# A graph-attention layer on one core: the edge stage works two steps ahead, with the masks prepared behind the copy of turned probabilities

## The chip, the cores and the metric

The kernel runs on one core of a Trainium2 chip. The core has five engines that run their own instruction streams and wait for each other through semaphores: TensorE (PE, matmuls and transposes into the PSUM banks), VectorE (DVE), ScalarE (ACT), GpSimd (POOL) and SyncE (SP, here for DMAs and counting). The metric is the device time of one execution in microseconds (us), as the median of several runs.

## What is computed

Cut to what matters:

```python
h = relu(layernorm(x))                       # x: 6250 x 256, float32
q, k, v = h @ wq + bq, h @ wk + bk, h @ wv + bv
scores = sum(q[dst] * k[src], -1) * scale + edge_weight * we + be   # 200000 edges, dst sorted
exp_s = exp(scores - segment_max(scores, dst)[dst])
attn = exp_s / segment_sum(exp_s, dst)[dst]
out = segment_sum(v[src] * attn[:, None], dst)
y = layernorm(h + out + h @ ws + bs)
y = layernorm(y + gelu(y @ w_ff1 + b_ff1) @ w_ff2 + b_ff2)
return x + y
```

The edges are sorted by destination. wk is folded into q and wv is applied after the sums, so that an edge needs only the row h[src].

## The kernel before

The kernel has three stages. The first normalises x, writes h to DRAM and builds q for 49 blocks of 128 nodes, each as three bfloat16 parts (`q3`). It also makes a table of steps. The third does wv, the residual, both layer norms and the feed-forward part.

Between them lies the edge stage. A chunk is 512 edges (J = 4 groups of 128 partitions), 392 chunks in all. A step is one pair of a chunk and a node block whose edges it holds; there are 440 steps here, run as 55 trips of U = 8 steps, written out in the loop body. Tiles that alternate are indexed by k = u % 2.

What each engine does for step s before the change (S, M, T, E name groups of TensorE's work):

- GpSimd gathers h rows by `src`, four indirect DMAs for each chunk (L488), into a ring of 8 slots (`rows`). SyncE counts landed chunks and, from `summed`, frees slots (L372).
- VectorE: `mark` (L705) writes `onehot[k]`, the 0/1 mask of edge against node, from the destinations. `edge_scores` (L832) multiplies the expanded q in banks 0 to 3 with the gathered rows and sums each row into a dot product, four instructions, then adds the edge term (L838). A custom instruction (L886) subtracts the mask from the scores spread in bank 4 and takes the maximum (`masked`, `new_max`). `add_sums` (L845) scales the running sums `acc` of the previous step's block and adds the new ones.
- ScalarE: `decay` and `probsT` are exponentials of `masked` (L618, L619). When TensorE has turned the probabilities, it copies them from banks 4 and 5 in two halves (L622). `prepare` (L585) turns `onehot[k]` into `outside`, 0 inside and -1e30 outside.
- TensorE: T turns `probsT` (L1066, 4 transposes), E expands q by the mask of step s+2 into banks 0 to 3 (L1011, 12 matmuls, in two halves), S spreads the scores of step s+1 into bank 4 (L1017, 4 transposes), M sums the rows of step s weighted by the probabilities (L1079, 4 float32 matmuls, which the profile shows as 8 passes).

Order in a step. TensorE: T, first half of E, S, second half of E, M. VectorE: masking of s, scores of s+1, keep the maximum, mark of s+3, read the old maximum (L709), add the sums of s-1. ScalarE: exp of s, two copies, prepare of s+2. S waits for the first of ScalarE's two copies (`probs_done`), since bank 4 holds half of the turned probabilities. The mark of s+3 waits until `outside_done` is at least s+2, which is the preparation of step s+1, one that ScalarE did in its step s-1.

Once per trip the residual projection of one block (`turn_h`, `copy_hTe`, `project_h`, `copy_r`, `store_r`) is done in the right half of bank 5. The order is the order of the code: each engine's queue is in order, and there is no scheduler.

Of the kernel before, what the change touches and what calls it, by code (L numbers as in the profile page):

```python
# [6 lines left out]
BF16 = mybir.dt.bfloat16  # L7
I32 = mybir.dt.int32
I16 = mybir.dt.int16
ALU = mybir.AluOpType  # L10
# [3 lines left out]
P = 128  # L14
# [8 lines left out]
BLOCKS = 64  # L23
# [10 lines left out]
def gnn_layer(nc, x, src, dst, edge_weight, wq, bq, wk, bk, wv, bv, ws, bs, we, be, g1, b1, g2, b2,  # L34
# [31 lines left out]
    ROUND = TP * BLOCKS + 1  # L66
    assert D == 2 * P and REST > 0 and FULL % 4 == 0 and B * P < PAD_DST and B < BLOCKS and S == G
# [3 lines left out]
    with ctx:  # L71
# [27 lines left out]
        stats = sb("stats", [P, NB, 6])  # L99
        mean = sb("mean", [P, NB])  # L100
        rstd = sb("rstd", [P, NB])
        nmr = sb("nmr", [P, NB])
        tmp = sb("tmp", [P, NB])
# [7 lines left out]
        ew_all = sb("ew_all", [P, R + J])  # L111
# [6 lines left out]
        WORK = 11120  # L118
# [148 lines left out]
        masked = part(C)  # L267
        probsT = masked
        probs = part(C).rearrange("p (j n) -> p j n", j=J)
        product = part(J * (D1 + 1) // 2, BF16).rearrange("p (j n) -> p j n", j=J)  # L270
# [3 lines left out]
        dots, score = (part(2 * J).rearrange("p (k j) -> p k j", k=2) for _ in range(2))  # L274
        old_max = part(2)
        new_max = part(1)
        decay = part(2)
# [6 lines left out]
        onehot_done, outside_done, q_edges, dotted, scored = sem("onehot_done"), sem("outside_done"), sem("q_edges"), sem("dotted"), sem("scored")  # L284
        spread, max_read, masked_done, max_kept = (sem(n) for n in ("spread", "max_read", "masked_done", "max_kept"))
        exp_done, turned, probs_done, summed, added = (sem(n) for n in ("exp_done", "turned", "probs_done", "summed", "added"))

        def counts(eng):
# [3 lines left out]
            n = eng.snap(regs[0], min_val=NW, max_val=TRIPS)  # L292
            m = eng.snap(regs[1], min_val=0, max_val=1)
            return n, m, eng.snap(regs[2], min_val=1, max_val=B)
# [10 lines left out]
        def block_of(eng, step):  # L305
            return eng.snap(eng.to_reg(step & (BLOCKS - 1)), min_val=0, max_val=B)

        def chunk_of(eng, step):
            return eng.snap(eng.to_reg(step >> (BLOCKS.bit_length() - 1)), min_val=0, max_val=B * TP + U)

        def slot_of(eng, chunk):
            return eng.snap(eng.to_reg(chunk & (S - 1)), min_val=0, max_val=S - 1)

        with nc.Block() as block:
            @block.sync
            def _(sp):
# [42 lines left out]
                with sp.Fori(0, rounds) as r:  # L359
                    with sp.Fori(0, NW) as i:  # L360
# [3 lines left out]
                        for u in range(G):  # L364
# [4 lines left out]
                            used_up = sp.to_reg(sp.snap(regs[u], min_val=1, max_val=T + B + S) + r * TP)  # L369
# [3 lines left out]
                            if u % WC == 0:  # L373
                                window = trip * 2 + (u // WC + 1)
                                before, marks = sp.to_reg(window * 16), sp.to_reg(sp.snap(regs[u + WC - 1], min_val=1, max_val=T + B + S) + r * TP)
# [7 lines left out]
                sp.sem_inc(chunk_landed, 1)  # L383
# [5 lines left out]
                all_back = sp.to_reg(sp.snap(all_turns, min_val=NW, max_val=B * NW) * 16 + 16)  # L389
                sp.wait_ge(late_in, 7 * 16)  # L390
                sp.wait_ge(r_copied, sp.to_reg(sp.snap(all_turns, min_val=NW, max_val=B * NW) + 1))
# [114 lines left out]
            def _(act):  # L506
# [51 lines left out]
                for b in range(B):  # L558
# [10 lines left out]
                    if b == 16:  # L569
                        act.wait_ge(ws_in, 3 * 16)  # L570
                        act.wait_ge(tab_turned, 3)
                        nc.scalar.activation(ew_all[:, R:R + J], banks[6][:, 0:J], ACT.Identity, bias=wb[:, 1:2], scale=wb[:, 0:1])
                        edge_terms(0, 512, 6, tab_copied)
                        edge_terms(512, 512, 7, tab_copied)
# [13 lines left out]
                nc.scalar.activation(decay[:, 1:2], eps[:, 0:1], ACT.Exp, scale=0.0).then_inc(sums_set, 1)  # L588
# [7 lines left out]
                def copy_hTe(turn):  # L596

                    act.wait_ge(hTe_ready, turn + 1)
                    nc.scalar.copy(hT_e, banks[5][:, D:2 * D]).then_inc(hTe_copied, 1)
                    act.dma_start(h_in, h_rows[bass.ds((turn + 1) % B * P, P), :]).then_inc(h_back, 16)  # L600

                def copy_r(turn):

                    act.wait_ge(r_stored, turn * 16 + 16)
                    act.wait_ge(r_ready, turn + 1)
                    nc.scalar.copy(r_out, banks[5][:, D:2 * D]).then_inc(r_copied, 1)

                def store_r(turn):

                    act.wait_ge(r_copied, turn + 2)  # L610
                    act.dma_start(r_rows[bass.ds(turn % B * P, P), :], r_out).then_inc(r_stored, 16)

                def trip(r, i, steps):
                    first = act.snap(act.to_reg(r * TP + i * U), min_val=0, max_val=B * TP)
                    for u in range(steps):
                        s, k = first + u, u % 2
                        act.wait_ge(masked_done, s + 1)
                        nc.scalar.activation(decay[:, k:k + 1], old_max[:, k:k + 1], ACT.Exp, bias=new_max, scale=-1.0)  # L618
                        nc.scalar.activation(probsT, masked, ACT.Exp, bias=new_max, scale=-1.0).then_inc(exp_done, 1)  # L619
                        for half in (1, 0):  # L620
                            act.wait_ge(turned, s * 2 + (2 - half))
                            nc.scalar.copy(probs[:, 2 * half:2 * half + 2, :].rearrange("p j n -> p (j n)"), banks[5 - half][:, 0:2 * P]).then_inc(probs_done, 1)  # L622
                        prepare(s + 2, k)
                        for at, body in ((3, copy_hTe), (6, copy_r), (7, store_r)):
                            if steps == U and u == at:
                                body(act.snap(act.to_reg(r * NW + i), min_val=0, max_val=B * NW))
# [5 lines left out]
            def _(dve):  # L632
# [57 lines left out]
                held = dve.alloc_register("block_of_last_step")  # L690
                steps_done = dve.alloc_register("steps_done")
                dve.reg_mov(held, B)
                dve.reg_mov(steps_done, 0)
                def place_of_mark(step):

                    chunk = chunk_of(dve, step)
                    there = dve.to_reg((chunk >> 2) * 16 + 16)
                    at = dve.snap(dve.to_reg((chunk & (G - 1)) * C), min_val=0, max_val=(G - 1) * C)
# [14 lines left out]
                def mark_first_steps():  # L713
# [6 lines left out]
                    nc.vector.memset(banks[7][:, 0:D1], 0.0).then_inc(sums_set, 1)  # L720
                    dve.load(regs[0:3], steps_tab[0:1, 0:3])
                    ahead[:] = [dve.snap(v, min_val=0, max_val=TP * BLOCKS) for v in regs[0:3]]
# [8 lines left out]
                for b in range(B):  # L731
# [44 lines left out]
                    if b == PLAN + 13:  # L776
# [19 lines left out]
                        nc.vector.scalar_tensor_tensor(out=steps_tab[0:1, :], in0=row(row_k), scalar=float(BLOCKS), in1=row(row_b), op0=ALU.mult, op1=ALU.add).then_inc(plan, 1)  # L796
# [8 lines left out]
                    if b == PLAN + 17:  # L805
# [4 lines left out]
                        nc.vector.tensor_scalar(free_row[0:1, 0:most], free_row[0:1, 0:most], float(S - 1), is_sorted[0:1, 0:1], ALU.add, ALU.mult).then_inc(plan, 1)  # L810
                        dve.wait_ge(plan, 12)
                        nc.vector.scalar_tensor_tensor(out=free_tab[0:1, :], in0=free_row[0:1, 0:most], scalar=1.0, in1=srow[0:1, 0:most], op0=ALU.add, op1=ALU.add).then_inc(plan_done, 1)
# [10 lines left out]
                def edge_scores(step, r, s, k, meanwhile=None):  # L823
                    chunk = chunk_of(dve, step)
                    slot = slot_of(dve, chunk)
                    column = dve.snap(dve.to_reg((chunk - r * TP) * J), min_val=0, max_val=R)
                    there, first_half, second_half = dve.to_reg(chunk + 1), dve.to_reg(s * 2 + 1), dve.to_reg(s * 2 + 2)
                    dve.wait_ge(chunk_landed, there)
                    for half, ready in ((0, first_half), (1, second_half)):
# [617 lines left out]
```

## Time and profile before

| | before |
|---|---|
| time, median of 3 runs | 2334.37 us (2331.2 to 2334.62) |
| profiled execution, span | 3211.3 us |
| PE busy | 2427.3 us (76%) |
| DVE busy | 1767.6 us (55%) |
| POOL busy | 1635.5 us (51%) |
| ACT busy | 1193.2 us (37%) |
| mean granted TensorE clock | 0.921 of full speed |

The profiled execution's own time is its span of 3211.3 us; it is 877 us longer than the median of the runs without a profile. Its parts must be read with that in mind: shares and durations of single instructions come from it, the total comes from the runs. PEld is TensorE's loading of weights, which overlaps the matmuls. "Idle before" is the time in which an engine stood ahead of an instruction, with what released it: "remote" and "issue" mean that the profile shows no work that ended then. The chain that ended last lies almost wholly in the third stage and tells nothing of the edge stage.

### The profile page before, as it was taken

To read this page: it belongs to the slowest core of one execution; us is meant where nothing else is said; L and a number is where in the kernel's file an instruction comes from. 1 tells how busy PE (TensorE), PEld (TensorE's weight loads), DVE (VectorE), ACT (ScalarE), POOL (GpSimd) and SP (SyncE) were. 2 spreads that over 40 slices of the span, in tenths; PEclk is the share of its full clock that TensorE was granted. 3 is DMA by queue.
4 is the path that set the end of the run, shared out by engine and by line. 5 is a ranking of instruction groups with operands and counts; after the bars stand their busy time and mean duration, and the time that the engine had idled before them with its cause. 6 is when DMAs were issued, how large, how long until landed. Compare 5 with 4: busy or idle time off the path is not lost. (4 is left out here: it accounts for less than half of the span.)

```text
span 3211.3 us, 68474 instructions
## 1 busy us (share of the span) xinstructions
PE 2427.3 (76%) x14747; PEld 1996.1 (62%) x14748; DVE 1767.6 (55%) x7372; ACT 1193.2 (37%) x2930; POOL 1635.5 (51%) x1828
## 2 busy tenths in 40 slices
PE   7577677777777777777777777777777777778998
PEld 5455556556555556565656566665666666657897
DVE  7454455555555545554555555555555555556787
ACT  6333333333333333333333333333333333334666
POOL 5355565555555545555554555555555445441154
PEclk8898899899899989998998999899988899999999
DMA  7233333333233323333233333332333233222222
GB/s 231 76 103 103 99 105 101 103 98 107 90 100 100 96 86 101 97 98 96 90 102 92 96 90 96 96 98 87 96 96 100 87 92 95 83 93 71 82 74 68
DMA packets 148148, 311.29 MB, mean 97 GB/s; under 512 B 33566, under 2 KB 84625, under 8 KB 148104
## 3 DMA queue, kind: packets, MB, share of 16 engines
q0 software_dynamic: 75264, 205.62, 21.5%
q1 hardware_dynamic: 54718, 90.19, 8.6%
q10 hardware_dynamic: 18122, 14.96, 1.5%
q8 instruction: 20, 0.33, 0.0%
q14 instruction: 24, 0.20, 0.0%
HBM read 290.21 MB, written 20.43 MB: 97 GB/s over the span
## 5 line engine op out<-in xcount | busy, mean ns | idle before, releaser
L488 POOL DMA_INDIRECT work<-h_rows,idx x1536 | 1457.3, 949 | 1339.9 <-SPq L372 956.2
L1079 PE MATMUL bank<-work 128*128 x3520 | 939.0, 412 | 24.5 <-issue 17.7
L1011 PE MATMUL bank<-q,onehot 128*128 x5304 | 804.6, 291 | 1.2 <-DVE work L832 0.7
L1079 PEld LDWEIGHTS bank<-work 128*128 128x128 f32 x3520 | 700.1, 211 | 146.8 <-issue 45.2
L886 DVE CUSTOM_DVE_ANT_0 work<-bank,work 128x512 f32<-128x512 f32 x440 | 330.5, 751 | 778.7 <-remote 476.4
L622 ACT COPY work<-bank 128x256 f32<-128x256 f32 x880 | 295.0, 376 | 1182.6 <-remote 812.8
L832 DVE SCALAR_TENSOR_TENSOR work<-bank,work 128x257 bf16<-128x257 f32 x1764 | 651.6, 425 | 143.5 <-PE bank L1011 44.2
L1017 PE MATMUL bank<-ident,work 128*128 128x128 f32 x1764 | 307.4, 302 | 500.5 <-ACT work L622 313.3
L1011 PEld LDWEIGHTS bank<-q,onehot 128*128 128x128 bf16 x5304 | 549.5, 104 | 85.4 <-issue 1.7
L1017 PEld LDWEIGHTS bank<-ident,work 128*128 128x128 f32 x1764 | 212.8, 148 | 578.0 <-ACT work L622 442.4
L1066 PE MATMUL bank<-ident,work 128*128 128x128 f32 x1760 | 283.6, 285 | 191.8 <-ACT work L619 182.8
L1066 PEld LDWEIGHTS bank<-ident,work 128*128 128x128 f32 x1760 | 214.8, 145 | 277.2 <-ACT work L619 230.6
L618 ACT ACTIVATE work<-work 128x1 f32<-128x1 f32 x440 | 129.5, 294 | 674.5 <-DVE work L886 550.3
L845 DVE SCALAR_TENSOR_TENSOR acc<-acc,work,bank 128x257 f32 x441 | 212.1, 481 | 230.4 <-remote 156.9
L619 ACT ACTIVATE work<-work 128x512 f32<-128x512 f32 x440 | 311.5, 708 | 0.0
L585 ACT ACTIVATE work<-onehot 128x512 bf16<-128x512 bf16 x442 | 282.9, 640 | 0.0
L705 DVE TENSOR_SCALAR onehot<-dst_words,node 128x512 bf16 x443 | 163.2, 368 | 72.5 <-issue 44.3
L832 DVE DVE_READ_ACCUMULATOR work<-bank,work 128x1 f32 x1764 | 145.0, 82 | 0.0
L838 DVE TENSOR_TENSOR work<-work,ew_all 128x4 f32<-128x4 f32 x441 | 72.5, 164 | 107.4 <-DVE work L832 43.5
L1405 PE MATMUL bank<-work,dst_words 128*128 128x128 f32 x784 | 96.0, 275 | 0.5 <-DVE work L1308 0.5
L1413 PE MATMUL bank<-dst_words,work 128*128 128x256 f32 x392 | 92.6, 379 | 0.0
L1405 PEld LDWEIGHTS bank<-work,dst_words 128*128 128x128 f32 x784 | 91.5, 192 | 1.2 <-issue 0.5
(195 smaller groups left out, 1519.5 us busy)
## 6 DMA issues: line engine op xcount, KB each, us to landing
dst_words<-dst_short SPq DMA_DIRECT2D x99, 512.0 KB
work<-h_rows,idx POOLq DMA_INDIRECT x1568
bias<-h_rows ACTq DMA_DIRECT2D x56, 128.0 KB
r_rows<-bias ACTq DMA_DIRECT2D x55, 128.0 KB
work<-r_rows SPq DMA_DIRECT2D x49, 128.0 KB, 2.3
h_rows<-acc SPq DMA_DIRECT2D x12, 512.0 KB, 6.6
work<-in_x SPq DMA_DIRECT2D x12, 512.0 KB, 3.5
out<-work SPq DMA_DIRECT2D x48, 128.0 KB, 1.7
```

Source lines behind the costliest of these rows:

```text
L488: pool.indirect_dma_start(rows[:, u, j, 0:D], None, h_rows, bass.IndirectOffsetOnAxis(idx[:, half, u * J + j:u * J + j + 1], 0)).then_inc( ...
L585: nc.scalar.activation(outside[:, k, :], onehot[:, k].rearrange("p j n -> p (j n)"), ACT.Copy, scale=BIG, bias=-BIG).then_inc(outside_done, 1)
L619: nc.scalar.activation(probsT, masked, ACT.Exp, bias=new_max, scale=-1.0).then_inc(exp_done, 1)
L622: nc.scalar.copy(probs[:, 2 * half:2 * half + 2, :].rearrange("p j n -> p (j n)"), banks[5 - half][:, 0:2 * P]).then_inc(probs_done, 1)
L832: last = nc.vector.scalar_tensor_tensor(out=product[:, j, 0:D1], in0=banks[j][:, 0:D1], scalar=SCALE, in1=rows[:, bass.ds(slot, 1), j, :], ...
L845: nc.vector.scalar_tensor_tensor(out=a, in0=a, scalar=decay[:, k:k + 1], in1=banks[6 + k][:, 0:D1], op0=ALU.mult, op1=ALU.add).then_inc(ad ...
L886: nc.vector.tensor_tensor_reduce(out=masked, in0=banks[4][:], in1=outside[:, k, :], scale=-1.0, scalar=old_max[:, k:k + 1], op0=ALU.add, o ...
L1011: last = nc.tensor.matmul(banks[j][:, 0:D1], onehot[:, k, j, :], q3[:, bass.ds(b, 1), c, 0:D1], start=(c == 0), stop=(c == 2))
L1017: last = nc.tensor.transpose(banks[4][:, j * P:(j + 1) * P], score[:, k, j:j + 1].broadcast_to([P, P]), ident[:])
L1066: last = nc.tensor.transpose(banks[5 - half][:, j * P:(j + 1) * P], probsT[:, (2 * half + j) * P:(2 * half + j + 1) * P], ident[:])
L1079: last = nc.tensor.matmul(banks[6 + k][:, 0:D1], probs[:, j, :], rows[:, bass.ds(slot, 1), j, :], start=(j == 2), stop=(j == 1))
L1405: last = nc.tensor.matmul(banks[2 + place(b)][:, m * P:(m + 1) * P], w1_sb[:, c, m * P:(m + 1) * P], unit_T[:, place(b), c * P:(c + 1) * P ...
```

## The change

The edge stage is reordered so that VectorE scores step s+2 and marks step s+4 in step s, and the sums of a step are made one step later and added one step later still.

- TensorE in step s: S of s+1 (waits for `masked_done` of s, no longer for the copies), second half of M of step s-1, T of s (all four transposes into bank 5), both halves of E for step s+3, first half of M of step s-1.
- VectorE: masking of s, scores of s+2, mark of s+4, add the sums of s-2. `q_edges` and `dotted` have one semaphore for each half. The mark waits for `outside_done` of at least s+3, the preparation of step s+2. Chunk and block sit the other way round in the step table, which takes some register instructions from the loop.
- ScalarE: exp of s, where due a part of the residual's copies, one copy of all 512 columns from bank 5, prepare of s+2.
- `masked`/`probsT` and `probs` have two buffers, `decay` four columns; `onehot` and `outside` keep two.
- The residual projection uses spare columns of banks 6 and 7, in halves of 128 columns: four short copies at u = 2, 3, 5, 6 instead of two, and VectorE waits for them ahead of `add_sums` there. Slots of gathered rows are freed one step later.

```diff
-        masked = part(C)
+        masked = part(2 * C).rearrange("p (k n) -> p k n", k=2)
...
                         act.wait_ge(masked_done, s + 1)
-                        nc.scalar.activation(decay[:, k:k + 1], old_max[:, k:k + 1], ACT.Exp, bias=new_max, scale=-1.0)
-                        nc.scalar.activation(probsT, masked, ACT.Exp, bias=new_max, scale=-1.0).then_inc(exp_done, 1)
-                        for half in (1, 0):
-                            act.wait_ge(turned, s * 2 + (2 - half))
-                            nc.scalar.copy(probs[:, 2 * half:2 * half + 2, :].rearrange("p j n -> p (j n)"), banks[5 - half][:, 0:2 * P]).then_inc(probs_done, 1)
+                        nc.scalar.activation(decay[:, u % 4:u % 4 + 1], old_max[:, k:k + 1], ACT.Exp, bias=new_max, scale=-1.0)
+                        nc.scalar.activation(probsT[:, k, :], masked[:, k, :], ACT.Exp, bias=new_max, scale=-1.0).then_inc(exp_done, 1)
+                        if steps == U and u in (2, 3):
+                            copy_hTe(act.snap(act.to_reg(r * NW + i), min_val=0, max_val=B * NW), u - 2)
+                        if steps == U and u in (5, 6):
+                            copy_r(act.snap(act.to_reg(r * NW + i), min_val=0, max_val=B * NW), 6 - u)
+                        act.wait_ge(turned, s + 1)
+                        nc.scalar.copy(probs[k][:].rearrange("p j n -> p (j n)"), banks[5][:]).then_inc(probs_done, 1)
                         prepare(s + 2, k)
...
-                        place, after_next = {}, dve.to_reg(s + 2)
+                        place, prepared = {}, dve.to_reg(s + 3)
...
-                        edge_scores(step_at(regs[u + 1]), r, s + 1, 1 - k, meanwhile)
+                        edge_scores(step_at(regs[u + 2]), r, prepared, k, meanwhile)
...
-                        dve.wait_ge(outside_done, after_next)
-                        mark(place[0], 1 - k)
+                        dve.wait_ge(outside_done, prepared)
+                        mark(place[0], k)
                         read_max(s + 1, 1 - k, block_at(u + 1))
-                        add_sums(s, 1 - k, dve.snap(held, min_val=0, max_val=B) if u == 0 else blocks[u - 1])
+                        if steps == U and u in (2, 3):
+                            dve.wait_ge(hTe_copied, dve.to_reg((r * NW + i) * 2 + (u - 1)))
+                        if steps == U and u in (5, 6):
+                            dve.wait_ge(r_copied, dve.to_reg((r * NW + i) * 2 + (u - 2)))
+                        add_sums(s, u + 2, dve.snap(held[u], min_val=0, max_val=B) if u < 2 else blocks[u - 2])
...
-                        pe.wait_ge(exp_done, s + 1)
-                        for half in (1, 0):
-                            for j in range(2):
-                                last = nc.tensor.transpose(banks[5 - half][:, j * P:(j + 1) * P], probsT[:, (2 * half + j) * P:(2 * half + j + 1) * P], ident[:])
-                            last.then_inc(turned, 1)
...
+                        pe.wait_ge(masked_done, s + 1)
+                        pe.wait_ge(scored, s + 2)
+                        spread_scores(1 - k)
+                        pe.wait_ge(probs_done, s + 1)
+                        sum_rows(1 - k, 1, slot)
                         pe.wait_ge(exp_done, s + 1)
+                        turn_probs(k)
+                        pe.wait_ge(onehot_done, s + (S + 4))
+                        pe.wait_ge(dotted[0], s + 3)
+                        expand_q(1 - k, 0, b)
+                        pe.wait_ge(dotted[1], s + 3)
+                        expand_q(1 - k, 1, b)
+                        sum_rows(1 - k, 0, slot)
```

How it moves instructions. TensorE before, from S of a step to T of the next (bank 4 is S, banks 2 and 3 the second half of E, bank 6 M, then T into banks 4 and 5):

```order
L1017 MATMUL bank4<-ident,work 128x128 [waits probs_done]
L1017 MATMUL bank4<-ident,work 128x128 x3
...
L1011 MATMUL bank2<-q3,onehot 128x257 [waits dotted]
L1011 MATMUL bank2<-q3,onehot 128x257 x2
L1011 MATMUL bank3<-q3,onehot 128x257 x3
...
L1079 MATMUL bank6<-work 128x257
...
L1079 ISA [waits probs_done]
...
L1066 MATMUL bank4<-ident,work 128x128 [waits exp_done]
```

TensorE after the change, the same stretch (L1052 is S, L1081 M, L1075 T, L1046 E):

```order
L1052 MATMUL bank4<-ident,mean 128x128 [waits scored,masked_done]
L1052 MATMUL bank4<-ident,mean 128x128 x3
L1081 ISA [waits probs_done]
L1081 MATMUL bank6<-work 128x257
L1081 ISA
L1081 MATMUL bank6<-work 128x257
L1075 MATMUL bank5<-ident,work 128x128 [waits exp_done]
```

S now waits for the masking instead of the copy, and between S and T stands half of M alone; E has moved behind T.

ScalarE before, one step (L618 and L619 exp, L622 the copies, L585 prepare):

```order
L618 ACTIVATE work<-work 128x1 [waits masked_done]
L619 ACTIVATE work<-work 128x512
L621 ISA
L622 COPY work<-bank4 128x256 [waits turned]
L621 REGISTER_ALU
L622 COPY work<-bank5 128x256 [waits turned]
L584 REGISTER_ALU
L585 ACTIVATE work<-onehot 128x512 [waits onehot_done]
```

ScalarE after, a step in which a part of the residual is copied (L637 and L638 exp, L616 the residual, L644 the copy, L601 prepare):

```order
L637 ACTIVATE mean<-mean 128x1 [waits masked_done]
L638 ACTIVATE work<-work,mean 128x512
L640 ISA
L616 COPY bias<-bank6 128x128 [waits hTe_ready]
L644 COPY work<-bank5 128x512 [waits turned]
L600 REGISTER_ALU
L601 ACTIVATE work<-onehot 128x512 [waits onehot_done]
```

Two copies have become one, and prepare stands behind it as before.

VectorE before, from the last of the scores to the next masking (L705 mark, L709 the old maximum, L845 the sums, L886 masking):

```order
L838 TENSOR_TENSOR work<-work,ew_all 128x4
L891 TENSOR_SCALAR neg_max<-work 128x1 [waits masked_done]
L705 ISA [waits dst_in,outside_done]
L705 TENSOR_SCALAR onehot<-dst_words,node 128x512
...
L709 TENSOR_SCALAR work<-neg_max 128x1
L842 REGISTER_ALU
L845 ISA [waits added,summed]
L845 SCALAR_TENSOR_TENSOR acc<-acc,work,bank7 128x257
```

VectorE after, the same place (L726 mark, L730 the old maximum, L868 the sums, L912 masking):

```order
L861 TENSOR_TENSOR mean<-mean,ew_all 128x4
L917 TENSOR_SCALAR neg_max<-mean 128x1 [waits masked_done]
L726 ISA [waits dst_in,outside_done]
L726 TENSOR_SCALAR onehot<-dst_words,node 128x512
L730 ISA [waits max_kept]
L730 TENSOR_SCALAR mean<-neg_max 128x1
L926 ISA
L865 REGISTER_ALU [waits hTe_copied]
L868 ISA [waits added,summed]
```

The rows stand in the same order with the same wait ahead of the mark; the number that it waits for has gone from s+2 to s+3, which only the diff shows.

## Rows read from the trace of the kernel before

**Rows 1.** Stretches: length, busy PE PEld DVE ACT POOL, PEclk, DMA share, GB/s

```profile
0.00:143.60 143.60, 92.61 (x460) 69.50 (x461) 85.47 (x257) 74.10 (x203) 66.80 (x96) 0.83 0.53 163
143.60:2951.00 2807.40, 2090.84 (x12686) 1704.90 (x12687) 1482.36 (x6597) 954.30 (x2310) 1467.77 (x1584) 0.92 0.31 95
2951.00:3211.30 260.30, 243.86 (x1603) 221.65 (x1601) 199.74 (x519) 164.79 (x419) 100.90 (x148) 0.98 0.25 81
...
2919.00:2943.00 24.00, 23.85 (x170) 20.99 (x169) 20.16 (x90) 12.78 (x31) 0.00 (x0) 1.00 0.11 35
```

**Rows 2.** Timeline, middle of the edge stage: start, length, engine, instruction, [idle before]

```profile
1510.56 0.94 POOL L488 DMA_INDIRECT work<-h_rows,idx  x1 [0.34 <-issue]
1511.81 0.95 POOL L488 DMA_INDIRECT work<-h_rows,idx  x1 [0.30 <-issue]
1512.66 0.37 ACT L622 COPY work<-bank 128x256 f32<-128x256 f32 x1 [3.98 <-remote]
...
1513.09 0.65 PE L1017 MATMUL bank<-ident,work 128*128 128x128 f32 x4 [3.03 <-issue]
```

**Rows 3.** Timeline of VectorE's masking, first and seventh of seven

```profile
2918.97 0.75 DVE L886 CUSTOM_DVE_ANT_0 work<-bank,work 128x512 f32<-128x512 f32 x1 [0.43 <-ACT work L585]
...
2943.03 0.75 DVE L886 CUSTOM_DVE_ANT_0 work<-bank,work 128x512 f32<-128x512 f32 x1 [0.24 <-PE bank L1017]
```

**Rows 4.** The gathers' line: duration min/median/max ns, first and last start, idle before

```profile
L488 POOL DMA_INDIRECT work<-h_rows,idx x1536: 940/947/1073, 150.5 to 2915.5; - x192
...
  SPq L372: 956.2, 319
  issue: 383.8, 1217
```

**Rows 5.** Timeline of the fastest pass from one masking to the next

```profile
994.71 0.75 DVE L886 CUSTOM_DVE_ANT_0 work<-bank,work 128x512 f32<-128x512 f32 x1 [1.93 <-ACT work L585]
995.39 0.08 DVE L886 DVE_READ_ACCUMULATOR2_ANT work<- 128x1 f32 x1
...
995.71 0.71 ACT L619 ACTIVATE work<-work 128x512 f32<-128x512 f32 x1
...
996.47 0.65 PE L1066 MATMUL bank<-ident,work 128*128 128x128 f32 x4 [0.83 <-ACT work L619]
...
996.94 0.65 ACT L622 COPY work<-bank 128x256 f32<-128x256 f32 x2 [0.53 <-PE bank L1066]
...
997.47 0.64 ACT L585 ACTIVATE work<-onehot 128x512 bf16<-128x512 bf16 x1
997.49 0.35 DVE L705 TENSOR_SCALAR onehot<-dst_words,node 128x512 bf16 x1
...
998.36 0.75 DVE L886 CUSTOM_DVE_ANT_0 work<-bank,work 128x512 f32<-128x512 f32 x1
```

**Rows 6.** Timeline of TensorE behind the last gather, where it never stands

```profile
2927.40 1.90 PE L1079 MATMUL bank<-work 128*128 x8
...
2929.14 0.60 PE L1066 MATMUL bank<-ident,work 128*128 128x128 f32 x4
...
2930.24 0.60 PE L1017 MATMUL bank<-ident,work 128*128 128x128 f32 x4
...
2930.68 0.83 PE L1011 MATMUL bank<-q,onehot 128*128 x6
```

**Rows 7.** Groups of ScalarE by form: count, busy us, mean ns, idle before

```profile
L622 ACT COPY work<-bank 128x256 f32<-128x256 f32 x880 | 295.0, 376 | 1182.6 <-remote 812.8 <-PE bank L1066 322.0 <-issue 46.7
...
L552 ACT ACTIVATE ew_all<-bank,wb 128x512 f32<-128x512 f32 x3 | 2.2, 783 | 0.0
...
L552 ACT ACTIVATE ew_all<-bank,wb 128x32 f32<-128x32 f32 x1 | 0.4, 378 | 0.0
```

**Rows 8.** Timeline of VectorE at a trip's end, mark and next masking

```profile
1607.41 0.35 DVE L705 TENSOR_SCALAR onehot<-dst_words,node 128x512 bf16 x1 [0.73 <-issue]
...
1608.75 0.75 DVE L886 CUSTOM_DVE_ANT_0 work<-bank,work 128x512 f32<-128x512 f32 x1 [0.43 <-issue]
```

More of the change, by code:

```diff
@@ L22 @@
 LEAD = 4
-BLOCKS = 64
+CHUNK_BITS = 15
+CHUNKS = 1 << CHUNK_BITS
 BIG = 1e30
@@ L821, in _, with edge_scores @@
                 third_part(B - 1)
-                def edge_scores(step, r, s, k, meanwhile=None):
+                def edge_scores(step, r, count, k, meanwhile=None):
                     chunk = chunk_of(dve, step)
-                    slot = slot_of(dve, chunk)
-                    column = dve.snap(dve.to_reg((chunk - r * TP) * J), min_val=0, max_val=R)
-                    there, first_half, second_half = dve.to_reg(chunk + 1), dve.to_reg(s * 2 + 1), dve.to_reg(s * 2 + 2)
+                    slot = slot_of(dve, step)
+                    column = dve.snap(dve.to_reg((chunk - r * TP) * J), min_val=0, max_val=R + J)
+                    there = dve.to_reg(chunk + 1)
@@ L828, in edge_scores @@
                     dve.wait_ge(chunk_landed, there)
-                    for half, ready in ((0, first_half), (1, second_half)):
-                        dve.wait_ge(q_edges, ready)
+                    for half in range(2):
+                        dve.wait_ge(q_edges[half], count)
                         for j in (2 * half, 2 * half + 1):
-                            last = nc.vector.scalar_tensor_tensor(out=product[:, j, 0:D1], in0=banks[j][:, 0:D1], scalar=SCALE, in1=rows[:, bass.ds(slot, 1), j, :],
+                            last = nc.vector.scalar_tensor_tensor(out=products[j][:, 0:D1], in0=banks[j][:, 0:D1], scalar=SCALE, in1=rows[:, bass.ds(slot, 1), j, :],
@@ L849, in _ @@
+                edge_scores(ahead[0], 0, 1, 0)
                 dve.wait_ge(outside_done, 1)
                 mark(place_of_mark(ahead[2]), 0)
+                edge_scores(ahead[1], 0, 2, 1)
+                dve.wait_ge(outside_done, 2)
+                mark(place_of_mark(ahead[3]), 1)
                 dve.wait_ge(sums_set, 2)
@@ L908, in _ @@
                     trip(0, n, HALF)
-                add_sums(dve.snap(steps_done, min_val=0, max_val=B * TP), 1, dve.snap(held, min_val=0, max_val=B))
+                for u in range(2):
+                    add_sums(dve.snap(steps_done, min_val=0, max_val=B * TP) + u, u + 2, dve.snap(held[u], min_val=0, max_val=B))
             @block.tensor
@@ new lines, in turn_probs, with sum_rows @@
+                def turn_probs(k):
+                    for j in range(J):
+                        last = nc.tensor.transpose(banks[5][:, j * P:(j + 1) * P], probsT[:, k, j * P:(j + 1) * P], ident[:])
+                    last.then_inc(turned, 1)
+                def sum_rows(k, half, slot):
+                    for j in (2 * half, 2 * half + 1):
+                        last = nc.tensor.matmul(banks[6 + k][:, 0:D1], probs[k][:, j, :], rows[:, bass.ds(slot, 1), j, :], start=(j == 2), stop=(j == 1))
+                    if half == 0:
+                        last.then_inc(summed, 1)
@@ new lines, in trip @@
+                        sum_rows(1 - k, 0, slot)
+                        slot = slot_of(pe, step_of[u])
+                        if steps == U and u in (1, 2):
+                            turn_h(pe.snap(pe.to_reg(r * NW + i), min_val=0, max_val=B * NW), u - 1)
+                        if steps == U and u in (4, 5):
+                            project_h(pe.snap(pe.to_reg(r * NW + i), min_val=0, max_val=B * NW), 5 - u)
+                    pe.reg_mov(slot_before, pe.to_reg(slot))
+                    pe.reg_mov(steps_done, pe.to_reg(first + steps))
```

223 lines of the change are left out of this document (120 added, 103 removed).

## The prediction

> **What bounds the kernel now.** I read first the table of stretches [rows 1]. The edge stage runs from 143.6 to 2951 us of the profiled execution and holds 440 steps: 2807.4 us, or 6.38 us a step. Before it lie 143.6 us, behind it 260.3 us, together 404 us. The profiled execution is much longer than the runs without a profile (3211.3 against a median of 2334.4 us), so the 6.38 us can't be the step that is timed. If the 404 us outside are the same in both, the timed step is (2334.4 - 404) / 440 = 4.39 us. That is the number the change has to beat.
>
> Why the profiled step is longer shows in the timeline. In the middle of the stage there are pauses in which ScalarE stands still for 3.98 us and TensorE for 3.03 us at the same time, while GpSimd goes on issuing gathers every 1.25 us [rows 2]. They are put down to "remote" or "issue", not to a wait of the kernel. Behind the last gather (2915.5 us) they are gone: between 2918.97 and 2943.03 us six steps take 24.06 us, or 4.01 us each, with TensorE busy for 23.85 of 24.00 us at the full 2.4 GHz [rows 1, 3]. So 4.0 us is TensorE's floor for a step, and there it is the bound.
>
> What then fills the timed 4.39 us? GpSimd issues 1536 gathers in the stage, one every 1.25 us where it doesn't wait: 0.947 us each and 383.8 / 1217 = 0.32 us between [rows 2, 4]. That makes 1920 to 1950 us, and the stage takes 1930 us in the timed runs. TensorE's floor is 440 x 4.0 = 1760 us. I read the timed stage as held by GpSimd's issue of gathers, with TensorE 0.4 us a step below it. In the profile GpSimd waits 956 us for free slots (released by SyncE) only because the pauses slow the others down.
>
> **The change, part by part.** Call the groups of TensorE's work in a step S (4 transposes that spread the scores), M (4 matmuls that sum rows, 8 passes), T (4 transposes of probabilities) and E (12 matmuls that expand q).
>
> First, S of the next step no longer stands behind the exponentials and their copy; it waits only for VectorE's masking (bank 4 is read). Before, one loop ran masking, exp, T, half of E, S, masking: the fastest pass in the trace takes 998.36 - 994.71 = 3.65 us [rows 5]. It goes. It was not the bound (4.0 and 4.39 are above it), so this saves nothing alone.
>
> Second, TensorE's work is the same in number: S, M, T, E, and the residual projection in other columns. Price nothing; its cover is its own slack if something else is slower.
>
> Third, VectorE scores step s+2 instead of s+1, and sums are added two steps late. Register instructions go from its loop. In the fast pass VectorE needs 3.65 us with hardly a gap, already under TensorE's 4.0. Saved: nothing on the path. A slot of gathered rows is freed one step later. The ring has 8 slots and a chunk is then held for 4 steps, so 4 steps (16 us and more) remain for a gather of 4 x 1.25 us: hidden, and with that cover gone it would cost up to one step per chunk.
>
> Fourth, the residual's copies are halved and stand on ScalarE between exp and the copy of turned probabilities, four of 128 columns in 8 steps instead of two of 256, each no dearer than the 0.376 us of 256 columns [rows 7]. They sit in the gap from exp's end (0.95 us behind the end of masking, below) to T's end (1.96 us): hidden. The VectorE waits for them are met long before. SyncE's doubled counts cost nothing. The drain at the end adds one M of 1.74 us [rows 6] and one sum, once.
>
> Fifth, and this is the part that decides: **the mask of step s+4 is written in step s, into the same two onehot buffers**. It must wait until ScalarE has prepared the mask of step s+2 from that buffer, and this preparation stands in ScalarE's step s, behind exp and behind the copy of turned probabilities. Before, the mask written in step s needed a preparation from ScalarE's step s-1: in the fast pass that ends at 998.11, and the mark that needs it comes 2.78 us behind 998.36, so 3.0 us ahead [rows 5]. Now every step closes this loop: masking, exp, T, copy, prepare, mark, masking of the next step. Queued behind the waiting mark on VectorE are the read of the old maximum, the add of the sums and the next masking, and for that masking ScalarE and TensorE wait.
>
> The loop, counted from the end of masking (995.39 + 0.08 = 995.47):
> - TensorE takes up S after 0.05 us (as T follows exp: 996.42 to 996.47 [rows 5]). S occupies it for 2930.68 - 2930.24 = 0.44 us, the first half of M for (2929.14 - 2927.40) / 2 = 0.87 us, T for 0.60 us [rows 6]. Exp is ready at 0.95 us (995.71 + 0.71 - 995.47), before T's turn at 1.36. T ends at 1.96 us.
> - ScalarE: 0.05 us to take up. One copy of 512 columns replaces two of 256. Two now start 0.27 us apart (0.65 together, 0.376 each). The rows of an activation from a bank, 783 ns for 512 columns and 378 for 32, give 0.84 ns a column [rows 7], so 256 more columns add 0.22 us: 0.49 us until prepare can start. Prepare lasts 0.64 us. It ends at 1.96 + 0.05 + 0.49 + 0.64 = 3.14 us.
> - VectorE: the wake-up of 0.05 us and a register instruction ahead of the mark, which the profile doesn't count. I put them at 0.15 us; it can't be under 0.05. Mark starts at 3.29 us. In the fast pass the mark started 2.02 us behind the end of masking (997.49), so VectorE now stands for about 1.3 us in every step.
> - Mark to the next masking: 998.36 - 997.49 = 0.87 us in an ordinary step, 1608.75 - 1607.41 = 1.34 us at a trip's end [rows 5, 8], on average 0.93 us. Masking itself: 0.76 us.
> - Sum: 3.29 + 0.93 + 0.76 = **4.98 us** a step.
>
> Against the profiled execution's own time this loop would, without pauses, give a stage of 440 x 4.98 = 2191 us inside it. Against the median: 404 + 2191 = **2595 us**, which is 2334.4 + 440 x 0.59.
>
> **Bounds of the unknown terms.** The copy: as cheap as one 256-column piece, 0.27 us, or as dear as the 512-column activation, 0.783 - 0.11 = 0.67 us. The VectorE take-up: 0.05 to 0.2. Low end 4.66 us a step: 404 + 2050 = 2454 us. The other open term is whether the timed runs hold a little of the pauses. If the 0.39 us between 4.0 and 4.39 are pauses that the timed runs have too, and not GpSimd's pace, they come on top of a chain that has no slack: 5.37 us, 404 + 2363 = 2767 us. TensorE's clock: in the stage it was granted 0.92 on average while it was busy 74% of the time; in the new loop it works 4.1 of 4.98 us. A clock of 0.92 would lengthen its 1.91 us in the loop by 0.15 us, 67 us in all, inside the range.
>
> **A rule against the trace.** The two 256-column copies let ScalarE begin when half of T is done: in the fast pass prepare starts 997.47 - 996.47 = 1.00 us behind T's start [rows 5]; with one copy it is 0.60 + 0.05 + 0.49 = 1.14 us. The Trainium skill, in Perfetto Trace Analysis, Optimizing Scalar/DVE Operations, says that where ScalarE isn't saturated but causes bubbles on others, breaking instructions up may finish the work sooner. The trace agrees as far as the 0.14 us go; by the rule two copies would give 2595 - 62 = 2533 us. The same skill, in ScalarE: Activation LUTs, Rules for kernel authors, budgets about 0.3 us for an activation and 0.83 ns for each element. An estimate from it makes prepare 0.72 us; the row here says 0.64, and the measurement decides. The sum would be 2630 us by the page.
>
> **Rivals.**
> - *Nothing changes* (2334 us): the loop is shorter than 4.39 us and GpSimd's pace holds both kernels. For it: 1920 us of gathers fit the timed stage closely. Against: 0.6 us of the loop would have to be missing, more than the low bounds give. Chance 0.06.
> - *Faster*: the preparation comes in time, the pace of GpSimd is not real without a profile, and TensorE's 4.0 us remains: 404 + 1760 = 2164 us, or anywhere up to 2320. It decides from a loop under 4.39 us. For it: the old loop through exp and S is gone. Against: the same 0.6 us, and in the old kernel that loop had slack anyway. Chance 0.05.
> - *Slower, with the timed runs' 0.39 us on top* (near 2767 us): same mechanism, other base. Chance 0.17.
> - *The clock falls*: TensorE idles 0.9 us in each step; were it granted 1.2 GHz throughout, its share of the loop doubles to 3.8 us, the step is 6.9 us, the time 3440 us. Against: the longest idle piece is short beside the pauses of 3 us after which the trace still averages 0.92. Chance 0.03.
> - *My forecast*, a step of 4.7 to 5.2 us, near 2595 us: chance 0.69.
>
> **Numbers.** Likeliest 2595 us. The range takes in both bounds: 2450 to 2770 us. A measurement of this kernel tells about 0.2% from no change. Slower by more: 0.69 + 0.17 + 0.03 = 0.89; within: 0.06; faster: 0.05.
>
> **What would show it.** In the new profile VectorE should sit idle ahead of its mark line, released by ScalarE's prepare line, for 1.2 to 1.3 us in each of 440 steps, some 550 us in all. TensorE should wait for the masking ahead of S, and GpSimd longer for SyncE. A stretch without pauses behind the last gather should show steps of 5.0 us with TensorE idle near 0.9 us. Ordinary fast steps there of 4.0 us, with no idle time ahead of the mark, would prove the loop wrong; steps of 5.4 us in the timed runs but 5.0 there would point to the pauses.

## The result, and the profile after

The changed kernel takes 2617.93 us (median of 4 runs, 2616.85 to 2618.66) against 2334.49 us before. The ratio is 1.1213, with a 95% interval of 1.1198 to 1.1227: 283 us slower. The forecast was 2595 us. One of the 14 runs of the kernel before that stand beside e1 to e4 took 2913.92 us at a granted clock of 0.718, and no ratio here counts it.

The profiled execution of the changed kernel has a span of 2616.9 us, as long as its runs without a profile. The stretches, cut where the edge stage begins and ends (columns as in [rows 1]: length, busy PE, PEld, DVE, ACT, POOL, granted clock, DMA share, GB/s):

```profile
0.00:116.80 116.80, 89.65 (x472) 68.93 (x473) 88.44 (x269) 73.96 (x204) 66.97 (x96) 0.93 0.66 200
116.80:2353.00 2236.20, 1900.06 (x12953) 1568.76 (x12953) 1408.57 (x6588) 920.54 (x1977) 1463.68 (x1584) 1.00 0.39 119
2353.00:2616.90 263.90, 246.82 (x1618) 224.21 (x1618) 201.53 (x530) 165.95 (x421) 100.93 (x148) 0.98 0.26 80
```

The edge stage takes 2236.2 us, 5.08 us a step. The pauses of [rows 2] are nowhere in it. They belonged to the one execution that was profiled for the kernel before; the profile of experiment e4, whose time is that of before, has none either. So the rows of before to compare with are those of e4 below, in which the stage is 1960.6 us, 4.46 us a step.

Who waits for whom in the changed kernel, the longest first (total us, times, longest):

```profile
ACT mean L637 <- DVE mean L912: 864.3, 440, 7.6
DVE onehot L726 <- ACT work L601: 662.6, 426, 1.6
POOL work L504 <- issue: 453.8, 1440, 1.6
ACT work L644 <- PE bank L1075: 439.1, 423, 1.3
PEld bank L1052 <- DVE mean L912: 385.0, 385, 1.3
PE bank L1052 <- DVE mean L912: 337.0, 440, 1.9
POOL work L504 <- SPq L388: 289.7, 96, 18.2
```

The second row is the loop: VectorE's mark (L726) waits for ScalarE's prepare (L601), 426 times, 662.6 us in all, 1.56 us each. ScalarE's exp then waits for the masking (first row), and so does TensorE's S (sixth). GpSimd, which hardly waits for slots in e4, stands 289.7 us for SyncE's free slots. One pass of the loop, from one end of masking (1507.97 + 0.08 = 1508.05) to the next masking, in the timeline of all engines (start, length, engine, instruction, [idle before]):

```profile
1507.97 0.08 DVE L912 DVE_READ_ACCUMULATOR2_ANT mean<- 128x1 f32 x1
...
1508.11 0.65 PE L1052 MATMUL bank<-ident,mean 128*128 128x128 f32 x4 [0.86 <-DVE mean L912]
1508.29 0.71 ACT L638 ACTIVATE work<-work,mean 128x512 f32<-128x512 f32 x1
...
1508.60 1.03 PE L1081 MATMUL bank<-work 128*128 x4
...
1509.47 0.60 PE L1075 MATMUL bank<-ident,work 128*128 128x128 f32 x4
...
1510.10 0.59 ACT L644 COPY work<-bank 128x512 f32<-128x512 f32 x1 [1.11 <-PE bank L1075]
...
1510.59 0.63 ACT L601 ACTIVATE work<-onehot 128x512 bf16<-128x512 bf16 x1
...
1511.39 0.35 DVE L726 TENSOR_SCALAR onehot<-dst_words,node 128x512 bf16 x1 [1.48 <-ACT work L601]
...
1512.24 0.75 DVE L912 CUSTOM_DVE_ANT_0 work<-bank,work,mean 128x512 f32<-128x512 f32 x1
```

Read it as a relay. S starts 0.06 us behind the end of masking, M at 0.55, T at 1.42 (exp was ready at 0.95). T ends at 2.02, the copy starts at 2.05, prepare at 2.54 and ends at 3.17. The mark starts at 3.34 after 1.48 us of idle time, the next masking at 4.19.

### The profile page after: what moved, and what is told of

Read it like the earlier page. It is cut to its first block and busy times, and to the rows that moved or that the text cites. A ratio compares the mean times of both kernels' runs of the same rounds, so it can differ in the third digit from the quotient of the medians.

```text
span 2616.9 us, 66636 instructions
## 1 busy us (share of the span) xinstructions
PE 2236.5 (85%) x15042; PEld 1861.9 (71%) x15043; DVE 1698.5 (65%) x7385; ACT 1160.5 (44%) x2601; POOL 1631.6 (62%) x1828
## 5 line engine op out<-in xcount | busy, mean ns | idle before, releaser
L1081 PE MATMUL bank<-work 128*128 x3528 | 910.9, 380 | 0.3 <-DVE acc L868 0.3
L1046 PE MATMUL bank<-q,onehot 128*128 x5316 | 663.3, 273 | 1.5 <-DVE norms L855 1.3
L1081 PEld LDWEIGHTS bank<-work 128*128 128x128 f32 x3528 | 603.2, 191 | 54.0 <-issue 0.7
L726 DVE TENSOR_SCALAR onehot<-dst_words,node 128x512 bf16 x444 | 157.2, 354 | 686.5 <-ACT work L601 662.6
L1052 PE MATMUL bank<-ident,mean 128*128 128x128 f32 x1764 | 286.5, 285 | 337.0 <-DVE mean L912 337.0
L1046 PEld LDWEIGHTS bank<-q,onehot 128*128 128x128 bf16 x5316 | 517.1, 97 | 69.1 <-issue 2.3
L1052 PEld LDWEIGHTS bank<-ident,mean 128*128 128x128 f32 x1764 | 180.8, 136 | 483.8 <-DVE mean L912 385.0
L637 ACT ACTIVATE mean<-mean 128x1 f32<-128x1 f32 x440 | 129.6, 294 | 864.3 <-DVE mean L912 864.3
L855 DVE SCALAR_TENSOR_TENSOR norms<-bank,work 128x257 bf16<-128x257 f32 x1326 | 492.8, 424 | 0.0
L644 ACT COPY work<-bank 128x512 f32<-128x512 f32 x440 | 258.2, 587 | 459.3 <-PE bank L1075 439.1
L912 DVE CUSTOM_DVE_ANT_0 work<-bank,work,mean 128x512 f32<-128x512 f32 x440 | 328.5, 747 | 26.5 <-issue 26.5
L638 ACT ACTIVATE work<-work,mean 128x512 f32<-128x512 f32 x440 | 311.6, 708 | 0.0
L601 ACT ACTIVATE work<-onehot 128x512 bf16<-128x512 bf16 x442 | 279.5, 632 | 0.0
L1075 PE MATMUL bank<-ident,work 128*128 128x128 f32 x1760 | 263.5, 272 | 0.0
L1075 PEld LDWEIGHTS bank<-ident,work 128*128 128x128 f32 x1760 | 218.4, 139 | 46.2
L868 DVE SCALAR_TENSOR_TENSOR acc<-acc,mean,bank 128x257 f32 x442 | 213.1, 482 | 50.6 <-issue 13.0
L855 DVE SCALAR_TENSOR_TENSOR work<-bank,work 128x257 bf16<-128x257 f32 x442 | 187.2, 424 | 6.8 <-SPq L384 0.6
L855 DVE DVE_READ_ACCUMULATOR norms<-bank,work 128x1 f32 x1326 | 109.6, 83 | 0.0
```

The source lines that it names most:

```text
L601: nc.scalar.activation(outside[:, k, :], onehot[:, k].rearrange("p j n -> p (j n)"), ACT.Copy, scale=BIG, bias=-BIG).then_inc(outside_done, 1)
L638: nc.scalar.activation(probsT[:, k, :], masked[:, k, :], ACT.Exp, bias=new_max, scale=-1.0).then_inc(exp_done, 1)
L644: nc.scalar.copy(probs[k][:].rearrange("p j n -> p (j n)"), banks[5][:]).then_inc(probs_done, 1)
L855: last = nc.vector.scalar_tensor_tensor(out=products[j][:, 0:D1], in0=banks[j][:, 0:D1], scalar=SCALE, in1=rows[:, bass.ds(slot, 1), j, :] ...
L868: nc.vector.scalar_tensor_tensor(out=a, in0=a, scalar=decay[:, u % 4:u % 4 + 1], in1=banks[6 + u % 2][:, 0:D1], op0=ALU.mult, op1=ALU.add) ...
L912: nc.vector.tensor_tensor_reduce(out=masked[:, k, :], in0=banks[4][:], in1=outside[:, k, :], scale=-1.0, scalar=old_max[:, k:k + 1], op0=A ...
```

## Experiments

Each kernel ran on the same chip as runs of the kernel before. Ratios are against those, with their 95% interval. The kernel before took 2338.7 us beside e1 to e4 and 2334.7 us beside e5 to e8, so a difference between two times of different sets is good to some 4 us.

### e1: prepare ahead of the copy

```diff
+                        prepare(s + 2, k)
                         act.wait_ge(turned, s + 1)
                         nc.scalar.copy(probs[k][:].rearrange("p j n -> p (j n)"), banks[5][:]).then_inc(probs_done, 1)
-                        prepare(s + 2, k)
```

> The changed kernel, with ScalarE's prepare of step s+2 moved ahead of the copy of turned probabilities (behind exp). Theory (the loop masking, exp, turn, copy, prepare, mark sets the 5.09 us step): prepare now ends 0.95 + 0.55 = 1.5 us behind the end of masking, before VectorE comes to its mark at 2.0 us, so the loop is gone; what is left is the larger of TensorE's 4.1 us a step (380 + 440 x 4.1 = 2184 us) and GpSimd's gathers, one per 1.25 us, 1536 of them: 117 + 7 + 1920 + 35 + 263 = about 2342 us. I expect 2320 to 2350 us, GpSimd hardly waiting for slots. Rival A (GpSimd's pace holds nothing): 2180 to 2220 us. Rival B (the loop is not what costs, but the deeper pipeline itself): stays near 2618 us.

Measured: 2349.68 us, ratio 1.0046 (1.0031 to 1.0061). Moving one line gives back 268 of the 283 us. That is inside the theory's range, at its upper end, and neither rival's. The time is that of the kernel before and a little more. Three rows of its waits:

```profile
ACT work L645 <- PE bank L1075: 387.4, 434, 1.7
DVE work L855 <- SPq L384: 247.0, 185, 3.2
...
DVE onehot L726 <- ACT work L601: 81.3, 105, 1.1
```

The mark's wait has fallen from 662.6 to 81.3 us. VectorE now waits where a chunk must have landed (L855, released by SyncE), 247 us. In the timeline the mark now follows the maximum (L917, which keeps it) after 0.06 us; ScalarE's prepare ended at 1504.50, 1.2 us ahead of the mark:

```profile
1503.87 0.63 ACT L601 ACTIVATE work<-onehot 128x512 bf16<-128x512 bf16 x1
...
1505.48 0.15 DVE L917 TENSOR_SCALAR neg_max<-mean 128x1 f32 x1
1505.69 0.35 DVE L726 TENSOR_SCALAR onehot<-dst_words,node 128x512 bf16 x1
```

### e2: T ahead of M

```diff
                         spread_scores(1 - k)
                         pe.wait_ge(probs_done, s + 1)
-                        sum_rows(1 - k, 1, slot)
                         pe.wait_ge(exp_done, s + 1)
                         turn_probs(k)
+                        sum_rows(1 - k, 1, slot)
```

> The changed kernel, with the turning of probabilities (T) put ahead of the half of the row sums (M) on TensorE. Theory: in the loop T starts when exp is ready, 0.95 + 0.05 us behind the end of masking, instead of at 1.42 us: the loop is 0.42 us shorter in each step, 5.09 - 0.42 = 4.67 us, time 2618 - 185 = 2433 us, still slower than before. Rival (the bound is TensorE's or ScalarE's total work, or GpSimd): no change, since the same instructions run; near 2618 us.

Measured: 2482.85 us, ratio 1.0619 (1.06 to 1.0638): 135 us faster than the changed kernel, 0.31 us a step, where 0.42 was expected. The work of TensorE is the same, so the rival falls. The missing 0.11 us stands in the timeline. Masking ended at 1509.11 + 0.09 = 1509.20:

```profile
1509.43 0.71 ACT L638 ACTIVATE work<-work,mean 128x512 f32<-128x512 f32 x1
...
1510.28 0.63 PE L1075 MATMUL bank<-ident,work 128*128 128x128 f32 x4 [0.38 <-ACT work L638]
...
1510.95 0.59 ACT L644 COPY work<-bank 128x512 f32<-128x512 f32 x1 [0.67 <-PE bank L1075]
```

Exp ends at 1510.14, and T starts 0.14 us later, not 0.05, and lasts 0.63 instead of 0.60. T ends at 1.71 us behind masking instead of 2.02: 0.31 us, what the step gained. The other steps of the trace have the same 0.14 and 1.71 us within 0.01.

### e3: prepare twice

```diff
+                        act.wait_ge(onehot_done, s + (S + 3))
+                        nc.scalar.activation(outside[:, k, :], onehot[:, k].rearrange("p j n -> p (j n)"), ACT.Copy, scale=BIG, bias=-BIG).then_inc(again, 1)
+                        act.wait_ge(again, s + 1)
                         prepare(s + 2, k)
```

> The changed kernel, with prepare done twice in each step, the second after the first has ended (an added cost on ScalarE of 0.63 + about 0.05 us per step). Theory: prepare is in the loop, so each step grows by all of it: 440 x 0.68 = 299 us, 2917 us. Rival (ScalarE, busy 44% of the time, has slack): no change.

Measured: 2955.37 us (2 runs, 2951.06 and 2959.69), ratio 1.2637 (1.2608 to 1.2666), 337 us slower than the changed kernel; 299 were expected. Every microsecond put on ScalarE at this point comes out in the time, though ScalarE was busy 44% of the span of the changed kernel. The 38 us beyond go with TensorE's clock. Two stretches of one step each, both the first step of a trip (columns as above, the clock third from the end), and the part of the first in which the clock was down:

```profile
1379.20:1386.50 7.30, 5.82 (x28) 4.58 (x28) 3.37 (x16) 2.65 (x5) 3.45 (x4) 0.77 0.25 72
1333.20:1339.00 5.80, 4.16 (x28) 3.38 (x28) 3.35 (x16) 2.65 (x5) 3.43 (x4) 1.00 0.34 100
...
1380.50:1383.90 3.40, 3.40 (x14) 2.73 (x13) 1.38 (x10) 0.76 (x2) 2.46 (x3) 0.51 0.41 116
```

With the same 28 matmul passes the step takes 7.3 us at a clock of 0.77 and 5.8 us at 1.00. Ahead of the slow one TensorE had stood idle for 2.06 us; then its half of M took 1.92 us instead of 1.03:

```profile
1380.14 0.84 PE L1056 MATMUL bank<-ident,mean 128*128 128x128 f32 x4 [2.06 <-DVE mean L916]
1380.78 1.92 PE L1085 MATMUL bank<-work 128*128 x4
```

For some 3.4 us it ran at 1.2 GHz instead of 2.4. The idle time alone doesn't decide it, for the fast step has the same ahead of it:

```profile
1334.11 0.65 PE L1056 MATMUL bank<-ident,mean 128*128 128x128 f32 x4 [2.05 <-DVE mean L916]
```

Counted over the whole trace, the clock is down in the first step of 35 of the 55 trips and in no other step of the stage. Those 35 steps take 6.94 us in the mean, the other 20 first steps 5.76: 35 x 1.18 = 41 us. The steps at full clock are 0.66 us longer than those of the changed kernel (5.75 against 5.09), 440 x 0.66 = 290 us. Together that is 331 us, and the profiled run was 333 us slower.

### e4: the kernel before with the packed step table

```diff
-            return eng.snap(eng.to_reg(step & (BLOCKS - 1)), min_val=0, max_val=B)
+            return eng.snap(eng.to_reg(step >> CHUNK_BITS), min_val=0, max_val=B)
...
-                    there = dve.to_reg((chunk >> 2) * 16 + 16)
+                    there = dve.to_reg((step & (CHUNKS - WC)) * (16 // WC) + 16)
```

> The kernel before, with the step table packed as in the change (block above, chunk below), which takes register instructions out of VectorE's loop; nothing else of the change. Theory (VectorE's loop is not the bound before): no change, 2334 us within 0.3%. Rival (VectorE's register instructions were on the path): faster by up to 0.1 us a step, 44 us. Its profile should also show whether the pauses of the first profile of before come back: if they belong to a profile of the faster pace, its span is far over its timed run again; if they were chance, the span is near the time.

Measured: 2336.75 us, ratio 0.9992 (0.9983 to 1.0002): no change. The shorter VectorE loop is worth nothing here. (The run also takes over from the change the masks laid on loaded counts, a few register instructions.) Its profile has a span of 2335.5 us and no pauses, and shows the old order as it is timed:

```profile
113.40:2074.00 1960.60, 1857.78 (x12670) 1585.51 (x12670) 1468.67 (x6586) 945.10 (x2305) 1475.18 (x1584) 0.99 0.46 136
0.00:113.40 113.40, 88.26 (x460) 68.05 (x461) 85.30 (x257) 73.99 (x203) 66.98 (x96) 0.92 0.68 206
2074.00:2335.50 261.50, 245.38 (x1620) 222.68 (x1618) 201.59 (x531) 166.29 (x422) 101.06 (x148) 0.98 0.26 81
```

The gathers' line in it, to set beside [rows 4]:

```profile
L494 POOL DMA_INDIRECT work<-h_rows,idx x1536: 945/949/1092, 121.8 to 2057.3; - x192
its engine sat idle before it (us, times) until:
  issue: 448.1, 1470
  SPq L378: 19.1, 19
```

GpSimd waits for slots only 19.1 us (956.2 in the paused execution). It issues almost without a break from 121.8 to 2057.3 us: 1535 intervals in 1935.5 us, 1.26 us each. And VectorE waits for landed chunks:

```profile
DVE work L837 <- SPq L374: 197.8, 148, 3.2
```

### e5, e6, e7: three of four gathers

```diff
-                    for j in range(J):
+                    for j in range(J - 1):
                         pool.indirect_dma_start(rows[:, u, j, 0:D], None, h_rows, bass.IndirectOffsetOnAxis(idx[:, half, u * J + j:u * J + j + 1], 0)).then_inc(rows_in[u][j], 16)
...
-                                sp.wait_ge(rows_in[u][j], landed)
+                                sp.wait_ge(rows_in[u][j], landed if j < J - 1 else 16)
```

In e5 on the kernel of e4:

> The kernel of before with the packed step table, and with three of the four gathers of each chunk from chunk 8 on (rows of the fourth group stay those of the first chunks, so that a quarter of the edges uses stale rows). GpSimd's pace falls from 5.0 to 3.76 us a chunk. Theory (before is held by GpSimd's gathers): the stage falls to TensorE's pace, 4.0 to 4.15 us a step by the steps that ran unhindered, 380 + 440 x 4.1 = 2184 us. Rival (the timed step of 4.4 us is made by the engines' own order and waits): no change, 2337 us.

Measured: 2203.31 us, ratio 0.9435 (0.9419 to 0.9451), 133 us faster than e4. So the gathers do bound the kernel before. The run takes out their issues and their DMA traffic alike; that it is GpSimd's issuing and not the traffic is read from the row above: GpSimd waits 19.1 us for slots, and a gather occupies it as long (median 949 ns) as in the changed kernel (946 ns), where less is moved in the same time (119 against 136 GB/s). The time is 19 us over the 2184 expected. What remains is TensorE: the stage is 1826.9 us, 4.15 us a step, with TensorE busy for 1809.46 us of it.

```profile
114.10:1941.00 1826.90, 1809.46 (x12668) 1589.16 (x12669) 1472.52 (x6586) 944.33 (x2305) 1111.10 (x1200) 1.00 0.39 118
```

In e6 on the kernel of e1:

> The changed kernel with prepare ahead of the copy, and with three of four gathers as above (a quarter of the edges uses stale rows). Theory: TensorE's work is the same, so it too goes to 4.0 to 4.15 us a step and 2170 to 2200 us; the deeper pipeline gives what the old one loses in waits at a trip's end, 0 to 40 us against the same kernel of before. Rival (VectorE's shorter loop of 3.5 us is worth something by itself): under 2100 us.

Measured: 2220.46 us, ratio 0.9507 (0.9491 to 0.9523). That is 20 us over the expected 2170 to 2200, and 17 us behind e5, where 0 to 40 us ahead were expected: with GpSimd out of the way, the deeper pipeline still gives nothing, and neither the theory's gain nor the rival's shows. In its list of waits the mark stands at ScalarE's prepare again, 201.1 us in 220 places, and ScalarE waits for the residual's parts (L625):

```profile
DVE onehot L726 <- ACT work L601: 201.1, 220, 1.1
ACT bias L625 <- PE bank L1069: 97.5, 110, 0.9
```

220 is four for each of 55 trips, and in the trace all of them fall in the steps u = 2, 3, 5 and 6, 55 in each: the steps in which a copy of the residual stands ahead of prepare. The copies weren't moved, so what they cost in time is not measured.

In e7 on the changed kernel as it is:

> The changed kernel as it is, with three of four gathers as above (a quarter of the edges uses stale rows). Theory (the loop through the copy and prepare sets the step, GpSimd has slack): no change, 2618 us within 0.5%. Rival (GpSimd or the DMAs have a part in the 5.09 us): faster by tens of us.

Measured: 2618.31 us (2617.97 and 2618.65), against 2617.93. With 384 gathers fewer nothing changes, and the stage is again 2236.2 us: neither GpSimd nor the gathers' traffic has a part in the 5.08 us.

### e8: prepare twice in the kernel before

The same edit as in e3, on the kernel of e4.

> The kernel of before with the packed step table, with prepare done twice in each step, one after the other (0.68 us more on ScalarE), as was done to the changed kernel. Theory: before the change a preparation was ready 3.0 us ahead of its mark, so all of it is hidden: 2337 us within 0.5%. Rival (ScalarE's work was on the path before as well): up to 299 us slower.

Measured: 2334.24 us, ratio 0.9998 (0.9988 to 1.0007). The 282.7 us of additional activations vanish:

```profile
L631 ACT ACTIVATE work<-onehot 128x512 bf16<-128x512 bf16 x440 | 282.7, 643 | 0.0
```

The same instruction costs 337 us in the changed kernel and nothing in the old one. That is the change's doing in one comparison: it put prepare on the path.

## Why the prediction was right

**The decisive step** was that the mark of step s+4 shares two buffers with step s+2, and so closes a loop through exp, T, the copy and prepare in one step. e1, e3 and e8 show it from three sides: take prepare out of the loop and 268 us go; add to it and all of it is paid; add the same before the change and nothing is paid. In the trace of e4 the preparation ends 3.0 us or more ahead of its mark in every step, as the prediction read it from one pass.

**The terms of the loop**, forecast against the means over the steps of the trace after: T's end 1.96 against 2.02 us, since M started 0.49 us behind S and not 0.44 (S takes 0.65 us where it follows a wait, and 0.60 in [rows 6], where it doesn't). Copy and prepare 1.18 against 1.15. The mark's take-up 0.15 against 0.18. Mark to masking 0.93 against 0.99, with 1.37 us in the last step of a trip. Masking 0.76 against 0.75. The sum was 4.98 and is 5.09 us: 0.11 x 440 = 48 us under the truth. The price of the 512-column copy, worked out from two rows of another activation [rows 7], was right: 0.59 us long and 0.48 to 0.49 us before prepare can start.

**The part outside the stage** was set at 404 us from the paused execution. It is 381 us after the change and 375 in e4: 143.6 us ahead of the stage [rows 1] had become 113.4 to 116.8. That is 23 us over the truth, and by luck it hides half of the error of the loop: 48 - 23 = 25 us, and 2595 was 23 us short. For the same reason the timed step of the kernel before was 4.46 us and not 4.39. The price of a lower clock was also a little off, 1.91 / 0.92 - 1.91 being 0.17 us and not 0.15, 73 us in all; it never came due.

**What bounded the kernel before**: GpSimd's gathers, read from 1.25 us a gather [rows 2, 4] and a timed stage of the same length. e5 shows it. TensorE's floor of 4.0 us came out as 4.15, since the six steps of [rows 3] are the first six of a trip of eight. The next one, in the same trace of before, takes 4.91 us (2943.03 to 2947.94):

```profile
2947.94 0.75 DVE L886 CUSTOM_DVE_ANT_0 work<-bank,work 128x512 f32<-128x512 f32 x1 [1.22 <-PE bank L1017]
```

**The rivals.** "Nothing changes" and "faster" both needed a loop under 4.39 us; it is 5.09. "The timed runs hold the pauses too" falls: the profiles without pauses have the spans of the timed runs. "The clock falls" did not happen at 5.09 us (granted 1.00 in the stage, with TensorE idle for 0.77 us a step ahead of S), but did in part at 5.8 us, in e3.

**The signs.** The idle time ahead of the mark was forecast at 1.2 to 1.3 us; it is 1.4 to 1.6 us, 662.6 us in all and not some 550. TensorE waits for the masking ahead of S, but stands (2236.2 - 1900.1) / 440 = 0.76 us a step and not 0.9, since it is busy for 4.32 us a step and not 4.1. GpSimd's waits for slots are longer than at the timed pace of before (289.7 against 19.1 us in e4), though shorter than in the paused execution (956.2).

**A rule.** The Trainium skill (Perfetto Trace Analysis, Optimizing Scalar/DVE Operations) says that where ScalarE isn't saturated but causes bubbles on others, breaking up instructions may let the work be finished sooner. Two smaller copies in place of the one would be that, and no run here shows it: in this layout both halves of T are in bank 5, and the first copy would have to run while TensorE writes that bank. The Trainium skill (ScalarE: Activation LUTs, Rules for kernel authors) gives its 0.3 us for an activation whose bias is an operand of one value for each partition. Prepare has its scale and bias as numbers in the instruction, so the prediction's 0.72 us, an estimate from that page, was made with a row for another form; the trace after says 0.63.

No run here with the full work is faster than the kernel before beyond the noise. e1, the nearest in which the change stands, is 11 us behind it and 13 us behind e4. Its gathers take as long as those of e4 (129.1 to 2065.2 us, 1936.1 us), but start 7 us later, and the stage runs 7 us longer behind the last one.

## What to carry to other kernels

Before deepening a pipeline, follow each buffer that isn't doubled with it: here the work went one step further ahead, the mask kept two buffers, and a wait with 3 us of slack became a loop closed in every step. What stands behind a wait in an in-order queue belongs to the loop, however idle its engine is (ScalarE was busy 44% of the span); moving one instruction ahead of that wait gave back 268 of 283 us. And look first for what really sets the pace: a queue of DMA issues at 1.25 us each, busy for three quarters of the stage by the count, left the whole change nothing to win.

## What the runs showed of the hardware

- A profiled execution can hold long pauses of ScalarE, VectorE and TensorE that lengthen it far beyond the timed runs beside it: 3211.3 us for a kernel that is timed at 2331.2 to 2337.04, while the nine other profiles of this study have spans within 7 us of their kernels' times. What was read between the pauses held: the pace of 1.25 us a gather [rows 2] and the terms of the loop [rows 5]. What caused the pauses stays open.
- In e3 an idle time of some 2.05 us of TensorE stands ahead of the first step of nearly every trip; in 35 of 55 trips 3.4 us at 1.2 GHz followed, in 20 none. What decides between them stays open. In the changed kernel, with waits of 0.77 us a step on average and 1.9 us at most ahead of S, the clock of the stage was 1.00.
- TensorE takes up T 0.05 us after exp in [rows 5], and 0.14 us after it in e2. Its idle time ahead of T doesn't explain that, being 0.83 us in the first and 0.38 us in the second; the cause stays open.
